# Residual added by accumulating transfers in HBM, and the homes of the token sums exchanged

## The reference

```python
xn = layernorm(x)
s = silu(xn @ w_gate.T)                    # 2752 features
s = where(s is among the half of its row with the smallest |s|, 0, s)
s = (s * (xn @ w_up.T)) @ w_down.T         # branch A
g = silu(((silu(xn @ W_gate.T)) * (xn @ W_up.T)) @ W_down.T)   # branch B
out = x + s * g
```

## Time and profile before

| | before |
|---|---|
| median of 3 runs | 2778.04 us |
| runs | 2775.75 to 2781.51 us |
| the profiled execution | 2776.88 us, its span 2775.1 us |
| granted TensorE clock, mean | 0.999 |
| HBM read and written | 492.31 and 120.59 MB |

### The profile page before, as it was taken

One profiled execution on the slowest core, in us unless ns is written; L12 is line 12 of the kernel. 1 busy time (PEld: TensorE's weight loads), 2 busy tenths in 40 slices (PEclk: granted clock), 3 DMA queues, 4 the chain that ended last, 5 costly groups with the idle time before them and its releaser, 6 DMA issues. The chain is left out here.

```text
span 2775.1 us, 31398 instructions
## 1 busy us (share of the span) xinstructions
PE 2747.3 (99%) x12204; PEld 2276.4 (82%) x12204; DVE 2303.4 (83%) x3002; ACT 1352.4 (49%) x1386; POOL 408.3 (15%) x185
## 2 busy tenths in 40 slices
PE   9999999999999999999999999999999999999999
PEld 7878888878788888888878888888887888888887
DVE  7676989999976798998986688999897767999971
ACT  4235988332445577731144457771115446776110
POOL 5555443074400000000020000000011000000000
PEclk9999999999999999999999999999999999999999
DMA  6898888579665555556665655555666664555564
GB/s 235 317 336 283 294 292 277 208 275 358 239 194 192 177 194 197 193 189 225 243 201 191 193 179 197 192 189 195 244 218 199 196 197 174 191 195 197 188 233 170
DMA packets 135097, 614.28 MB, mean 221 GB/s; under 512 B 12752, under 2 KB 12752, under 8 KB 89168
## 3 DMA queue, kind: packets, MB, share of 16 engines
q1 hardware_dynamic: 134992, 612.94, 63.1%
HBM read 492.31 MB, written 120.59 MB: 221 GB/s over the span
## 5 line engine op out<-in xcount | busy, mean ns | idle before, releaser
L632 PE MATMUL ps<-w_split,hid_ring 128*128 128x512 f32 x4096 | 934.1, 390 | 6.3 <-POOL w_split L1209 4.3
L632 PEld LDWEIGHTS ps<-w_split,hid_ring 128*128 128x128 f32 x4096 | 769.0, 188 | 170.3 <-issue 5.4
L1383 DVE TENSOR_SCALAR_CACHE_REDUCE ranks<-key_buf,cand 128x2752 int16<-128x2752 f32 x248 | 762.9, 3076 | 5.8
L961 ACT ACTIVATE signs_row<-key_buf,cand 128x2752 bf16<-128x2752 f32 x248 | 642.2, 2590 | 191.0 <-DVE cand L1392 181.5
L877 PE MATMUL ps<-xnT,w_split 128*128 128x512 f32 x1376 | 535.3, 389 | 0.0
L876 PE MATMUL ps<-xnT,w_split 128*128 128x512 f32 x1376 | 535.3, 389 | 0.0
L875 PE MATMUL ps<-xnT,w_split 128*128 128x512 f32 x1376 | 535.3, 389 | 0.0
L1209 POOL TENSOR_TENSOR w_split<-w_raw,w_split 128x1024 fp32r<-128x1024 f32 (+3 forms) x142 | 310.2, 2197 | 351.2 <-ACT w_split L928 126.3
L876 PEld LDWEIGHTS ps<-xnT,w_split 128*128 128x128 f32 x1376 | 258.3, 188 | 53.7
L875 PEld LDWEIGHTS ps<-xnT,w_split 128*128 128x128 f32 x1376 | 258.3, 188 | 53.6
L877 PEld LDWEIGHTS ps<-xnT,w_split 128*128 128x128 f32 x1376 | 258.3, 188 | 53.4
(11 more groups left out here) (146 smaller groups left out, 2892.2 us busy)
## 6 DMA issues: line engine op xcount, KB each, us to landing
w_split<-split SPq DMA_DIRECT2D x272, 1024.0 KB, 4.8
split<-w_split SPq DMA_DIRECT2D x72, 1024.0 KB, 6.6
w_raw<-w_a SPq DMA_DIRECT2D x100, 512.0 KB, 4.3
w_raw<-t_dram SPq DMA_DIRECT2D x78, 512.0 KB, 3.4
w_raw<-w_b SPq DMA_DIRECT2D x42, 512.0 KB, 4.6
w_extra_raw<-t_dram SPq DMA_DIRECT2D x42, 512.0 KB, 4.0
t_dram<-t_buf SPq DMA_DIRECT2D x20, 1024.0 KB, 8.7
w_extra_raw<-w_a SPq DMA_DIRECT2D x30, 512.0 KB, 3.7
```

The lines of the kernel that those rows point to most:

```text
L632: ins = pe.matmul(ps[:, 2 * t + half, :], h, w[:, half * TB:(half + 1) * TB], start=(first and n == 0), stop=last and stop)
L961: act.activation(signs_row[:, :], keys[:, t, :], ACT.Sign, bias=cand_f[:, t:t + 1], scale=-1.0, accum_out=counts[:, t:t + 1]).then_inc(act ...
L1383: dve.tensor_scalar(ranks[:, :], keys[:, t, :], cand_f[:, t:t + 1], 0.0, ALU.is_lt, ALU.add, accum_out=counts[:, t:t + 1]).then_inc(sel_st ...
```

## The change

In blocks 0 to 2 SyncE copies each tile of `x` straight to its place in the output, from HBM to HBM, at the point in its order where it loaded it into `x_res`. GpSimd then issues one transfer for each `t`, once that copy has landed and VectorE has multiplied the tile; it adds `silu_g` to what stands in the output (`accum_op`) and counts up `added`. The three additions on GpSimd, the one on VectorE and the four stores on SyncE fall away. The first two sums (P6, P5) now lie over `x_res`, which these blocks no longer load, and wait for nothing but their own input; the last two (P7, P3) lie over `silu_g` and wait for `added`. Block 3 adds and stores as before.

```diff
--- before.py
+++ after.py
@@ -58,6 +58,8 @@
 T1, T3, T4, T2 = range(4)
+
+S_HOME = (2, 3, 0, 1)
@@ -392,6 +394,7 @@
         stored = sem("stored")
+        added = sem("added")
@@ -440,7 +443,6 @@
             sp.sem_inc(tiles_done, RING)
-            sp.sem_inc(stored, 16)
@@ -553,14 +555,8 @@
                     t = m - AD0 - 4 - NT
-                    sp.dma_start(x_res[:, t, :], x_v[b][:, t, :]).then_inc(xres_landed[t], 16)
-
-            def store(b, t):
-                if t < OUT_POOL:
-                    sp.wait_ge(out_ready, b * OUT_POOL + (t + 1))
-                else:
-                    sp.wait_ge(out_last, b * (NT - OUT_POOL) + (t - OUT_POOL + 1))
-                sp.dma_start(out_v[b][:, t, :], x_res[:, t, :]).then_inc(stored, 16)
+                    dst = out_v[b][:, t, :] if b < NB - 1 else x_res[:, t, :]
+                    sp.dma_start(dst, x_v[b][:, t, :]).then_inc(xres_landed[t], 16)
@@ -570,11 +566,6 @@
                             spill(TILES - 4 + a)
-                        if a == W_RING - 1:
-                            store(b - 1, 0)
-                            store(b - 1, 1)
-                        elif W_RING <= a < W_RING + 2:
-                            store(b - 1, a - W_RING + 2)
                 for m in range(0 if b == 0 else B0, TILES):
@@ -597,15 +588,16 @@
                 if t < OUT_POOL - 1:
-                    sp.wait_ge(out_ready, (NB - 1) * OUT_POOL + (t + 1))
+                    sp.wait_ge(out_ready, t + 1)
                 else:
-                    sp.wait_ge(out_last, (NB - 1) * (NT - OUT_POOL) + 1)
+                    sp.wait_ge(out_last, 1)
                 sp.dma_start(out_v[NB - 1][:, t, :], x_res[:, t, :]).then_inc(stored, 16)
...
                 cols = slice(half * TB, (half + 1) * TB)
-                sp.wait_ge(out_last, (NB - 1) * (NT - OUT_POOL) + (half + 2))
+                sp.wait_ge(out_last, half + 2)
                 sp.dma_start(out_v[NB - 1][:, NT - 1, cols], x_res[:, NT - 1, cols]).then_inc(stored, 16)
-            sp.wait_ge(stored, 16 * (NT * NB + 1) + 16)
+            sp.wait_ge(added, (NB - 1) * (16 * NT))
+            sp.wait_ge(stored, 16 * (NT + 1))
@@ -806,7 +798,7 @@
                         which = (P6, P5, P7, P3).index(p)
-                        return s_split[:, which, part, 2 * (1 - pair) + n, at_col:at_col + P]
+                        return s_split[:, S_HOME[which], part, 2 * (1 - pair) + n, at_col:at_col + P]
                     half, first = {P4: (1, STAGE * P), P1: (0, 0), P2: (1, 0)}[p]
@@ -1023,21 +1015,18 @@
                     act.wait_ge(s_raw, (b - 1) * 4 + 4)
-                    act.activation(s_split[:, which, 0, :, :].rearrange("p k n -> p (k n)"), prods[:, which, 0:H], ACT.Copy).then_inc(s_high, 1)
+                    act.activation(s_split[:, S_HOME[which], 0, :, :].rearrange("p k n -> p (k n)"), prods[:, which, 0:H], ACT.Copy).then_inc(s_high, 1)
...
                             if a == 1:
-                                act.wait_ge(out_ready, (b - 1) * OUT_POOL + STAGE)
                                 s_hi(0)
                             elif a == 2:
-                                act.wait_ge(out_ready, (b - 1) * OUT_POOL + OUT_POOL)
-                                act.wait_ge(out_last, b)
                                 s_hi(1)
                             elif a == 5:
-                                act.wait_ge(stored, b * (16 * NT) + 16)
+                                act.wait_ge(added, b * (16 * NT))
                                 s_hi(2)
@@ -1063,7 +1052,8 @@
-                act.wait_ge(stored, b * (16 * NT) + 16)
+                if not first_block:
+                    act.wait_ge(added, b * (16 * NT))
@@ -1257,7 +1247,13 @@
                         s_sum(b + 1, n)
-                for t in range(OUT_POOL if b < NB - 1 else OUT_POOL - 1):
+                if b < NB - 1:
+                    for t in range(NT):
+                        pool.wait_ge(xres_landed[t], b * 16 + 16)
+                        pool.wait_ge(ad_free, b * NT + (NT + t + 1))
+                        pool.dma_start(out_v[b][:, t, :], silu_g[:, t, :], accum_op=ALU.add).then_inc(added, 16)
+                    continue
+                for t in range(OUT_POOL - 1):
                     pool.wait_ge(xres_landed[t], b * 16 + 16)
@@ -1402,7 +1398,6 @@
                         xn_low(b, n)
-                    last_outputs(b - 1, OUT_POOL)
@@ -1452,8 +1447,8 @@
                     dve.wait_ge(s_high, (b - 1) * 4 + (which + 1))
-                    dve.tensor_tensor(s_split[:, which, 1, :, :].rearrange("p k n -> p (k n)"), prods[:, which, 0:H],
-                                      s_split[:, which, 0, :, :].rearrange("p k n -> p (k n)").bitcast(F32), ALU.subtract).then_inc(s_ready, 1)
+                    dve.tensor_tensor(s_split[:, S_HOME[which], 1, :, :].rearrange("p k n -> p (k n)"), prods[:, which, 0:H],
+                                      s_split[:, S_HOME[which], 0, :, :].rearrange("p k n -> p (k n)").bitcast(F32), ALU.subtract).then_inc(s_ready, 1)
```

## The result

| | before | after |
|---|---|---|
| median of 5 runs | 2778.04 us | 2795.11 us |
| lowest and highest | 2775.75 to 2781.51 us | 2792.73 to 2795.54 us |
| ratio | | 1.0052, 95% interval 1.0041 to 1.0063 |
| span of the profiled execution | 2775.1 us | 2793.6 us |

The account below looks back on a forecast made before the run. TensorE was taken as the bound, busy 2747.3 of 2775.1 us; 4.4 us of its waits for VectorE would go and all else was priced at nothing: 2778.0 - 4.4 = 2773.6 us, range 2770 to 2798.

Parts of the forecast that it names:

- the 4.4: Three block changes: TensorE waits less for VectorE's last token chunks, 1.45, 1.5 and 1.5 us, in sum 4.4 us won.
- the 1.5 and 1.6 that the range allowed for: Possible extra gains, not counted: 1.5 us of small waits for `s_split`, 1.6 us of lowered clock at the third change.
- the paragraph on the accumulating transfers: Block changes: GpSimd's four transfers land at 742 to 745, before ScalarE's third high half needs them; hidden, cost nothing.
- that deadline: ScalarE's third high half: accumulations landed by 749.6, 18.6 us after the first is issued; each us beyond costs TensorE one.
- Tile 8's chain: Before P5: tile 8's transfer, two conversions, second sum's low half; moves along with TensorE, its 1.5 us of waits remain.
- the third rival: Block changes: issuing holds VectorE up, or tile 8's load lengthens, 1.5 us a change, cancelling the win; 2778 us, 17%.
- the lower part: Accumulations at a plain store's price: four take 5.2 to 6 us of engine time and stay hidden.
- the second rival: Accumulations cost load plus store, land about 755, TensorE idle at P7, 4 us a change; 2790 us, 38%.
- Its other half: Issuing the transfers occupies GpSimd and the shared way into SBUF, so L1348 still takes 2.5 us at block changes.
- the upper bound: Accumulations as load then store, one after the other: 15.5 us, 2793.5; lowered clock 1.6 x 3 more, 2798.

Follow-up runs that it names:

- the last version with the additions on VectorE: The kernel before with GpSimd's additions moved to VectorE, the second sum's low half behind tile 5's, SyncE's stores two loads further back: 2782.26 us, ratio 1.0014.
- the last version of the changed kernel: The changed kernel, second sum's low, third's both, fourth's high half before tile 8's, whose low half follows P6's first two uses: 2774.31 us, ratio 0.9985.
- the second sum early: The changed kernel with the second sum's low half on VectorE behind tile 5's low half instead of tile 8's: 2784.13 us, ratio 1.0012.

## Why the prediction was wrong

*What held.* TensorE's largest wait came from GpSimd's additions stretching two low halves: 6.6 to 2.3 us against 6.6 to 2.1 forecast, the pair in 1.29 us. In the last version with the additions on VectorE, which has no new transfers, the pair takes 1.28 us, so it is the absence of GpSimd's additions that frees it. The kernel without the transfers gains 6.1 to 13.6 us by its interval; the 4.4 with the 1.5 and 1.6 that the range allowed for are 7.5, which lies in it, but I did not take the gain apart. The copies in HBM are free, as argued (6.2 us to landing against 6.1).

*The step that failed* is the paragraph on the accumulating transfers: it asked whether they land before ScalarE wants the third high half, "hidden up to 746.6 + 3.0 = 749.6, which is 18.6 us after the first is issued; every us beyond costs TensorE one". But that deadline was not the first one. ScalarE came to the third high half only at 754.22, 20.5 us after TensorE's first tile, and found the accumulations landed. No run tests the deadline with loads that are in time; the nearest measure is the last version of the changed kernel, where they had landed 19.1 us after that tile, which by the prediction's own rule is 0.5 us of loss a change and not 5. What was late were the loads of tiles 6, 7 and 8, which ScalarE and VectorE convert in this order, the second sum's low half behind them. Tile 8's chain (transfer, high half, low half, second sum) stood in the same prediction, priced at nothing with "unless the transfer gets quicker or slower" and in the third rival called without slack; that tiles 6 and 7 stand ahead of it in the chain it did not count, having priced tile 6's load as one that nobody waits for. The transfers made tile 8's load 9.7 us (743.58 to 753.26) instead of 4.7: I let the loads keep their 46 to 54% of the engines and gave the accumulations the rest, and did not ask what the accumulations leave to the loads. By engine time they leave little. The DMA queues of the changed kernel, 733 to 753 us (packets, MB, share of 16 engines):

```profile
q0 software_dynamic: 576, 2.10, 59.6%
q1 hardware_dynamic: 814, 2.80, 38.5%
...
w_extra_raw<-t_dram SPq DMA_DIRECT2D x2, 512.0 KB, 10.3
```

and of the kernel before in the same stretch, 731 to 751 us:

```profile
q1 hardware_dynamic: 1523, 5.14, 76.1%
...
w_extra_raw<-t_dram SPq DMA_DIRECT2D x2, 512.0 KB, 4.5
```

GpSimd's queue had 59.6% and the loads 38.5%, and tiles 6 and 7 took 10.3 us to land instead of 4.5. From 737 to 741 us, when tile 6's load should have come in, it was 94.9% against 7.4%.

*The engine time.* I took "the lower part", a plain store's price, since the store was the nearest row. Measured: 2.8 us of all engines against 1.4, twice the store, which is what the second rival supposed. The Trainium skill (Collectives: The Full Stack, "Why ReduceScatter is half of AllGather") gives two source reads and a factor of two for the reducing step of a ring of ranks. The pages of the profile agree on the factor for this transfer: 1.2% against 0.6%. That it is the second read they do not show: both queues count 6.29 MB, and HBM read is 492.31 MB with the adding and without.

*The rivals.* The second had the engine time of the transfers right and nearly the time (2790), with the wrong wait: it expected TensorE idle at P7 and ScalarE waiting for a transfer into `out`; it is idle at P5 and ScalarE waits for loads. The third named the right chain and priced it at 1.5 us a change; it measured 5.0. Its other half, that issuing such transfers would hold VectorE up, is refuted: with one being issued at 737.66 the pair at 737.03 took 1.29 us. Neither counted the clock rightly: the 1.6 us a change stood only in the upper bound, and it was 1.5 to 2.9 at every change.

That it takes both, late loads and this order, is shown by two runs: the last version of the changed kernel has the same transfers and loads as late, in another order, with 0.67% between the two ratios, some 19 us less; and the kernel before with the second sum moved shows no difference.

## What to carry to other kernels

A new transfer has two victims: whoever waits for it, and whoever waits for what it shares the DMA engines with. Follow the second as far as the first; here a chain with no slack ran through loads whose tiles were not needed yet (tile 8's, issued when tile 2 is done, is needed five tiles of 2.8 us later, 14 us), only because their conversions stood ahead of one that was needed. Where a load may come late, keep conversions that do not depend on it ahead of it in the engine's order; that costs nothing while it is in time and was worth 11 us of 14 here by one moved line. And price a wait of some us on a busy TensorE with its clock: 5.3 to 5.6 us idle cost here another 1.5 to 2.9.

## What the hardware showed

An accumulating transfer of 512 KB from SBUF into HBM took 2.8 us of all 16 DMA engines, a plain one from the same queue 1.4. With loads beside them they landed after 11.0 and 6.5 us (medians of 12). Issuing one kept GpSimd for 0.87 us, a plain one for 0.53. In competition, from 733 to 753 us, GpSimd's accumulating queue got more of the engines than SyncE's loads, 59.6 to 38.5%, and moved less, 2.10 to 2.80 MB.

TensorE's clock fell to 1.2 GHz behind all three waits of 5.3 to 5.6 us of the changed kernel, and behind one of the three waits of 2.1 to 2.5 us of the kernel before. In "the second sum early" it fell behind the waits of 3.15 and 3.02 us (24 matmuls in 7.30 and 7.32 us) and not behind that of 2.86 (5.71); in the kernel without GpSimd's transfers it fell behind one of 2.36 us (7.37). So the length of the wait alone did not decide it.
